# Attention over sixteen wavelengths with routed experts: moving one exponential to VectorE, the wavelength weights, a store order and a bias addition

## The reference

```python
xn = layernorm(x)
Q, K, V = (xn @ W + b for each of q, k, v), split into 16 heads of 8
for wl in range(16):                                  # wavelengths
    m = cos(phase_modulators[wl])                     # per head
    scores = (Q * m) @ (K * m).T / sqrt(8)
    scores = scores * cos(KERR * scores * scores)
    acc += softmax(scores) @ V * interference_weights[wl]
attention = (acc / 16) @ Wo + bo
# experts: each token goes to its best expert, if that has room
probs = softmax(xn @ gate_w.T)
expert_out[e] = relu(tokens_of_e @ w1[e] + b1[e]) @ w2[e] + b2[e]
out = x + attention + probs_of_choice * expert_out
```

## Time and profile before

| what | value |
|---|---|
| time, median of 3 runs | 1809.99 us (1807.09 to 1810.4) |
| the profiled execution | 1809.65 us, span 1807.9 us |
| ACT busy | 1726.9 us, 96% of the span |
| DVE busy | 1526.0 us, 84% |
| PE busy | 1490.7 us, 82% |
| POOL busy | 157.6 us, 9% |
| mean granted TensorE clock | 0.986 |
| exponentials of 128 x 4096 | 482, 3626 ns each |
| tails of 128 x 1024 on ScalarE | 8, 1041 ns each |

### The profile page before, as it was taken

The page is one execution under the profiler, slowest core; times in us unless marked ns, Lnnn a source line. Parts: engine busy times, 40 slices in busy tenths (PEclk is TensorE's granted clock), DMA queues, the critical chain, the costliest instruction groups (busy, mean ns, idle before and its releaser), DMA issues. The chain is left out here.

```text
span 1807.9 us, 45710 instructions
## 1 busy us (share of the span) xinstructions
PE 1490.7 (82%) x20014; PEld 942.5 (52%) x20014; DVE 1526.0 (84%) x2554; ACT 1726.9 (96%) x533; POOL 157.6 (9%) x168
## 2 busy tenths in 40 slices
PE   4797888777899999999997787777787787778877
PEld 2364544544556666656664454444455555445555
DVE  8445887889898888988888999999988998898785
ACT  3699999999999999999999999999999999999995
POOL 6200111110000000000000131332000000000000
PEclk9799999999999999999999999999999999999998
DMA  6000111000011110111000000000000000000001
GB/s 207 21 15 15 37 49 43 23 25 15 22 36 42 42 43 20 31 36 43 22 22 15 18 12 25 23 25 19 15 2 15 15 15 15 15 15 2 8 13 31
DMA packets 44999, 50.07 MB, mean 28 GB/s; under 512 B 6725, under 2 KB 37359, under 8 KB 44799
## 3 DMA queue, kind: packets, MB, share of 16 engines
q1 hardware_dynamic: 42463, 42.91, 7.5%
q0 software_dynamic: 2048, 4.20, 0.7%
q10 hardware_dynamic: 288, 0.00, 0.0%
HBM read 30.96 MB, written 15.73 MB: 26 GB/s over the span
## 5 line engine op out<-in xcount | busy, mean ns | idle before, releaser
L1044 ACT ACTIVATE Pr<-T 128x4096 f32<-128x4096 f32 x482 | 1694.3, 3626 | 17.7 <-PE bank L924 16.9
L924 PE MATMUL bank<-Pr,Vst 128*32 128x256 f32 x15424 | 936.7, 383 | 249.6 <-ACT Pr L1044 140.9
L924 PEld LDWEIGHTS bank<-Pr,Vst 128*32 128x32 f32 x15424 | 520.2, 110 | 546.8 <-issue 343.8
L866 DVE COPY T<-bank 128x512 f32<-128x512 f32 x252 | 172.4, 684 | 82.9 <-PE bank L860 82.9
L850 DVE TENSOR_REDUCE negmax<-bank 128x2 f32<-128x512 f32 x256 | 164.1, 681 | 30.1 <-PE bank L844 28.7
L1015 PE MATMUL bank_b<-terms,ident 128*128 128x128 f32 x1024 | 150.3, 280 | 0.8 <-DVE terms L1003 0.7
L965 DVE SCALAR_TENSOR_TENSOR d_mantissa<-d_mantissa 128x1024 f32<-128x1024 f32 x108 | 147.0, 1361 | 0.0
L968 DVE SCALAR_TENSOR_TENSOR shared<-shared,d_scaled 128x1024 f32<-128x1024 f32 x108 | 140.0, 1297 | 0.0
L1015 PEld LDWEIGHTS bank_b<-terms,ident 128*128 128x128 f32 x1024 | 130.3, 192 | 16.0 <-issue 9.1
L971 DVE SCALAR_TENSOR_TENSOR shared<-d_mantissa,shared 128x1024 f32<-128x1024 f32 x108 | 132.0, 1222 | 2.9
L963 DVE SCALAR_TENSOR_TENSOR shared<-d_mantissa 128x1024 f32<-128x1024 f32 x108 | 130.9, 1212 | 0.0
(11 more groups left out here) (175 smaller groups left out, 911.1 us busy)
## 6 DMA issues: line engine op xcount, KB each, us to landing
Ks<-qk_parts SPq DMA_DIRECT2D x31, 288.0 KB
Qs<-qk_parts SPq DMA_DIRECT2D x93, 96.0 KB
work<-in_L_ffn_w_dram SPq DMA_DIRECT2D x16, 256.0 KB, 3.5
qk_parts<-Pr SPq DMA_DIRECT2D x8, 384.0 KB, 2.7
qk_parts<-work SPq DMA_DIRECT2D x8, 384.0 KB, 2.8
dispatched<-T SPq DMA_DIRECT2D x5, 512.0 KB, 4.9
region<-dispatched SPq DMA_DIRECT2D x8, 320.0 KB, 3.5
expert_out<-work SPq DMA_DIRECT2D x8, 320.0 KB, 2.4
```

What stands on the lines that cost most here:

```text
L866: nc.vector.tensor_copy(T[par][:, ds(p * BANK, BANK)], sc_bank[rr][:, :]).then_inc(sc_read, 1)
L924: ins = nc.tensor.matmul(bank[VC * j:VC * (j + 1), half * SEQ:(half + 1) * SEQ], Vst[par][:, at:at + VC], moving, start=opens and half == ...
L1044: nc.scalar.activation(Pr[n % RING][:, :], T[par][:, :], ACT.Exp, scale=scales[u % 2][w]).then_inc(exp_done, 1)
```

## The change

1. `D_CHUNKS` is 4 in the units with an expert too. ScalarE's tail falls away there, VectorE gets seven more operations, and the products of wavelength 15 move behind the next unit's first products.
2. The wavelength weights go into the copies. A column of row_weight holds, for one group, 16 in each row of sums and the weight in each row of totals; row_scale is its reciprocal. The copy to pv_s becomes a multiplication by that column, the gain operation falls away. row_weight is filled at the start by GpSimd and by 16 small DMAs from ScalarE's queue.
3. SyncE issues the last part's store of units 2 and 3 after the next stack's load.
4. GpSimd adds the bias bo to base in four operations behind the first two stagings, no longer in the combine.

```diff
+    FIRST_OF = (0, 3, 6, 8, 11, 14)
+    LAST_OF = (2, 5, 7, 10, 13, 15)
...
+                    pool.memset(row_weight[:, :], float(W)).then_inc(weight_room, 1)
                     pool.memset(one_col[:, :], 1.0).then_inc(root_table, 1)
...
                     act.dma_start(bk_s[:, :], bk.rearrange("(d a) -> d a", a=1)).then_inc(bias_in, 16)
+                    act.wait_ge(weight_room, 1)
+                    for w in range(W):
+                        q = GROUP_OF[w]
+                        row = (w - FIRST_OF[q]) * OC + HD
+                        act.dma_start(row_weight[row:P:VC, q:q + 1], weights.rearrange("(a w) -> a w", a=1)[:, w:w + 1].to_broadcast([GR, 1])
+                                      ).then_inc(row_weight_in, 16)
...
+                    dve.wait_ge(row_weight_in, 16 * W)
+                    nc.vector.reciprocal(row_scale[:, :], row_weight[:, :])
...
+            def pool_output_bias(pool):
+
+                pool.wait_ge(xn1_ready, SIDE_TILES)
+                for c in range(CHUNKS):
+                    b = base[:, c * CH:(c + 1) * CH, :]
+                    nc.gpsimd.tensor_tensor(b, b, bo_s[:, :].unsqueeze(1).to_broadcast([P, CH, D]), ALU.add).then_inc(biased, 1)
...
             def pool_combine(pool, c):
-                nc.gpsimd.tensor_tensor(base[:, s, :], base[:, s, :], bo_s[:, :].unsqueeze(1).to_broadcast([P, CH, D]),
-                                        ALU.add).then_inc(pool_comb, 1)
+                pool.wait_ge(biased, CHUNKS)
                 pool.wait_ge(gathered[c], 16 * CH)
...
-                nc.vector.tensor_copy(pv_s[q % 2][:, :], pv_bank[q % 2][:, :]).then_inc(pv_copied, 1)
+                nc.vector.tensor_scalar(pv_s[q % 2][:, :], pv_bank[q % 2][:, :], row_scale[:, q:q + 1], None, ALU.mult).then_inc(pv_copied, 1)
...
-                nc.vector.tensor_tensor(gain[:, 0:size, :], rsum[:, 0:size, :], weight, ALU.mult).then_inc(gain_ready, 1)
-                dve.wait_ge(gain_ready, n + 1)
...
-                                        gain[:, 0:size, :].unsqueeze(3).to_broadcast([P, size, OTW, HD]), ALU.mult).then_inc(terms_ready, 1)
+                                        rsum[:, 0:size, :].unsqueeze(3).to_broadcast([P, size, OTW, HD]), ALU.mult).then_inc(terms_ready, 1)
...
-            D_CHUNKS = [{FIRST: 0, SECOND: 2, PLAIN: 4, EXPERT: 3, FINAL: 4}[KINDS[u // 2]] for u in range(UNITS)]
+            D_CHUNKS = [{FIRST: 0, SECOND: 2, PLAIN: 4, EXPERT: 4, FINAL: 4}[KINDS[u // 2]] for u in range(UNITS)]
...
                 for u in range(2):
                     stage_v(pool, u, u)
+                pool_output_bias(pool)
...
-                for u in range(2, 4):
+                for u in range(2, 5):
                     j = (u - 2) * NQ_SIDE
                     sp.wait_ge(sc_made, pair_no(u, 0))
                     load_stack(sp, u + 2, u % 2)
-                    sp_side1(sp, j, j + NQ_SIDE - 1)
+                    if u > 2:
+                        sp_side1(sp, j - 1, j)
+                    if u < 4:
+                        sp_side1(sp, j, j + NQ_SIDE - 1)
                     load_rows(sp, u + 2, u % 2)
-                    sp_side1(sp, j + NQ_SIDE - 1, j + NQ_SIDE)
-                for u in range(4, EU):
+                for u in range(5, EU):
                     unit(u, u % 2)
```

More of the change, by code:

```diff
@@ L71, in attention_and_experts @@
     RING = 2
+    FIRST_OF = (0, 3, 6, 8, 11, 14)
+    LAST_OF = (2, 5, 7, 10, 13, 15)
+    GROUPS = len(FIRST_OF)
+    GROUP_OF = tuple(sum(w > last for last in LAST_OF) for w in range(W))
     DCOLS = 4 * SEQ
@@ L144, in attention_and_experts @@
         rsum = sb("rsum", [P, SLOTS, OTW])
-        gain = sb("gain", [P, SLOTS, OTW])
+        row_weight = sb("row_weight", [P, len(FIRST_OF)])
+        row_scale = sb("row_scale", [P, len(FIRST_OF)])
         terms = [sb(f"terms{i}", [P, SLOTS, OTW * HD]) for i in range(2)]
@@ L229, in attention_and_experts @@
             proj, part1, rest1, part2, part3 = (ssem(n) for n in ("proj", "part1", "rest1", "part2", "part3"))
-            v_made = ssem("v_made")
+            v_made, weight_room, row_weight_in = ssem("v_made"), ssem("weight_room"), ssem("row_weight_in")
             angle, sine = ssem("angle"), ssem("sine")
@@ L508, in attention_and_experts @@
                 "v_staged", "exp_done", "pv_done", "pv_copied", "turned"))
-            inverted, gain_ready, terms_ready, terms_summed, summed = (asem(n) for n in (
-                "inverted", "gain_ready", "terms_ready", "terms_summed", "summed"))
+            inverted, terms_ready, terms_summed, summed = (asem(n) for n in (
+                "inverted", "terms_ready", "terms_summed", "summed"))
             exp_table, t0_copied, d_step, whole_done = asem("exp_table"), asem("t0_copied"), asem("d_step"), asem("whole_done")
@@ L518, in attention_and_experts @@
                 "route", "gate_in", "gate_exp", "mask_ready", "index_ready"))
-            scattered, pool_comb, base_ready = asem("scattered"), asem("pool_comb"), asem("base_ready")
+            scattered, pool_comb, base_ready, biased = asem("scattered"), asem("pool_comb"), asem("base_ready"), asem("biased")
             gathered = [asem(f"gathered{c}") for c in range(CHUNKS)]
@@ L773, in pool_combine @@
                 s = slice(c * CH, (c + 1) * CH)
-                nc.gpsimd.tensor_tensor(base[:, s, :], base[:, s, :], bo_s[:, :].unsqueeze(1).to_broadcast([P, CH, D]),
-                                        ALU.add).then_inc(pool_comb, 1)
+                pool.wait_ge(biased, CHUNKS)
                 pool.wait_ge(gathered[c], 16 * CH)
                 nc.gpsimd.tensor_tensor(got[:, s, :], got[:, s, :], over(r[:, 0, s], D), ALU.mult).then_inc(pool_comb, 1)
-                pool.wait_ge(pool_comb, 2 * (c + 1))
+                pool.wait_ge(pool_comb, c + 1)
                 nc.gpsimd.tensor_tensor(base[:, s, :], base[:, s, :], got[:, s, :], ALU.add).then_inc(base_ready, 1)
@@ L994, in dve_turned @@
                 slots = tr_bank[:, :].rearrange("p (a c) -> p a c", c=VC)[:, :, 0:size * OC].rearrange("p a (s c) -> p s a c", c=OC)
-                weight = over(iw_s[:, FIRST_OF[q]:LAST_OF[q] + 1], OTW)
                 dve.wait_ge(turned, n + 1 + 2)
@@ L1048, in stage_v @@
                                       .rearrange("p (t d) -> p t d", d=HD)).then_inc(v_staged, 1)
[L1052 to L1055, removed]
             COPY_AT = {3: 0, 6: 1, 8: 2, 11: 3, 14: 4, 17: 5}
@@ L1244, in plain_scalar @@
             def plain_scalar(act):
-                nc.scalar.activation(gain[:, 0, 0:1], one_col[:, :], ACT.Exp).then_inc(exp_table, 1)
+                nc.scalar.activation(rsum[:, 0, 0:1], one_col[:, :], ACT.Exp).then_inc(exp_table, 1)
                 for q in range(0, SIDE_B, 2):
```

## The result

The changed kernel takes 1786.38 us (median of 4 runs, 1786.15 to 1787.72) beside 1809.91 us for the kernel before (4 runs): ratio 0.9875, 95% interval 0.9858 to 0.9892. It is faster by 23.5 us; 20 were forecast, and the range 1784 to 1800 holds it. The profiled execution took 1786.21 us, its span 1784.5.

A forecast was written before the change was run, and what follows sets the result against it. Bound by ScalarE's exponentials, plus a start, an end and 24.7 us of breaks. 8.0 + 6.7 + 0.4 + 6.5 - 1.3 - 0.2 = 20.1 off 1809.99 gave 1789.9, written as 1790 us; range 1784 to 1800.

The forecast's parts named there:

- Stores behind loads: Units 3 and 4: loading the stack ahead of the store closes ScalarE's waits of 3.73 and 4.30 us; gain 8.0 us.
- Bias early: Combines: without GpSimd's bias addition, all four ScalarE breaks from 1105 us on go; gain 6.7 us.
- Rival 2: Combines: GpSimd's multiplication and addition still block VectorE, so the four breaks stay; 1796.6 us, chance 0.07.
- The bias at the start: Start: GpSimd's four bias additions delay VectorE's split of the row maxima, and so ScalarE's third exponential; cost 1.3 us.
- Sixteen DMAs at no cost: Setup: sixteen issues take 7.4 us, within ScalarE's 7.77 us idle before its first root; no cost, 0.4 us of cover spare.
- rival 3: Setup: the sixteen DMAs take 1.09 us each, making the first root 9.7 us late; 1799.6 us, chance 0.10.
- the prediction's own signs of being wrong: VectorE busy throughout an expert unit with TensorE waiting, first root after 11 us, or VectorE steps of several us under the combine.
- The whole last wavelength: Eight expert units: ScalarE's 1.04 us tail and 0.21 us wait go, a new 0.5 us wait comes at seven boundaries; gain 6.5.
- The total in front of them is the same: Expert unit boundaries: TensorE's reordered work ahead of the second products takes equally long, so a 0.5 us wait appears.
- rivals 1 and 4: Expert units: 1, VectorE binds, 1796.4 us, chance 0.14; 4, VectorE's 7.67 us idle does not shrink, 1843 us, chance 0.08.
- The end: Last two groups, behind the last exponential: VectorE's chain gets shorter through the weights in the copies; gain 0.4 us.
- The copies: VectorE, each group: the copy of 0.68 us becomes a multiplication by a per-partition scalar, 0.07 us more.

The follow-up runs named there:

- the reversal: The changed kernel with one part taken back: for the stores, SyncE's old order, 1795.42 us; for the last wavelength, three VectorE chunks in expert units, 1794.39 us.
- two kernels with the same start: The kernel before (1809.91 us) and the changed kernel with the weights where they were (1786.87 us); same code up to GpSimd's bias addition at 57.4.
- second profile: The changed kernel run once more without any change, as yardstick for three later kernels: 1786.86 us.
- the fourth kernel above: The changed kernel with DMA issues and reciprocal moved later, bias addition delayed, and 4, 2, 3, 3 chunks on VectorE in units 0 to 3: 1780.88 us.

## Why the prediction was right, point by point

- **Stores behind loads: 8.0 forecast.** 8.24 by the reversal. The load was forecast for 8.0 us before its unit's first exponential and went out 9.8 before it.
- **Bias early: 6.7.** All four breaks went, as forecast, and the bias did it alone. The term was a little small: the first exponentials of two such units stood 54.55 us apart (1159.75 - 1105.20 in the trace before), 1.9 more than fifteen exponentials of 3.51, while I counted the 1.72 that shows. Rival 2 (the two other instructions block as before) fell. The forecast's reason held for the step that it looked at: that step finds GpSimd idle, which waits for the gathered rows until 1112.62, and takes 1.22 us. The Trainium skill's SBUF — State Buffer (SBUF: two separate sides, under Who interferes with whom), which stands behind rival 2, is borne out all the same: the step at 1113.83 ends 1.1 us after GpSimd's multiplication does (1115.07). What the forecast and the rival both lacked is how long GpSimd works without a gap: bias and multiplication together had none, multiplication and addition have one, and so the two that are left block for 1.1 and 0.8 us and not for 3.9 and 2.2.
- **The bias at the start: -1.3.** The bias alone cost 0.90 (the wait ahead of the third exponential was 1.35 instead of 0.45); that the third exponential came 1.28 later in all, with 0.38 from the first in it, and so near 1.3, is chance. VectorE's cast of the maxima, 0.17 us, took 1.38, until GpSimd's addition ended at 67.50:

```profile
58.23 9.27 POOL L556 TENSOR_TENSOR base<-base,bo_s 128x1024 f32<-128x1024 f32 x4
...
66.15 1.38 DVE L893 CAST nm_parts<-negmax 128x16 bf16<-128x16 f32 x1
```

- **Sixteen DMAs at no cost.** This step was wrong in size. An issue took 0.57 us (9.14 / 16), not 0.45, so the first root came at 12.35 instead of 11.01: the cover of 0.4 us was gone, as rival 3 had it, but by 1.3 us and not by 9.7. A first root later than 11 us was one of the prediction's own signs of being wrong, and it came. Most of the 1.3 was taken up by later waits of the setup; the first exponential was 0.38 later, with the new reciprocal in it, for which 0.2 had been charged, and within the 0.46 by which two kernels with the same start differ (62.98 and 62.52, above). The 14 issues at 46.83 took 0.53 each with no issue of SyncE beside them, so most of the price is the issue's own. The Trainium skill's Perfetto Trace Analysis (Per-instruction lifecycle: what the profiler-reported window actually captures) has the generator locked by each issue; the runs do not clearly show that as a delay of SyncE: its three loads of x took 3.15 to 4.13 us in the five executions with the sixteen beside them and 3.01 to 3.45 in the five without.
- **The whole last wavelength: 6.5.** 7.63 by the reversal. The mechanism was right, wait and place included; the size of the new wait was off, 0.20 to 0.21 instead of 0.5. "The total in front of them is the same" failed: the same pieces take TensorE 0.29 us less in the new order. VectorE's busy time was 51.14 of 52.96 us where 52.1 was estimated, and its idle time shrank from 7.67 to 1.8: rivals 1 and 4 fell. With the gain in the chain it is 52.00, and 0.3 us of the wait at the boundary is left, so rival 1 was close.
- **The end: 0.4.** VectorE's chain there is 0.41 us shorter, as forecast. The span shows 1.26 (23.32 before, 22.06 after); the end varies by more than that from one execution to the next, see below.

The copies cost what was forecast, 0.741 us instead of 0.679 (0.06 more, forecast 0.07).

The forecast was 3.6 us too high: 1.1 from the last wavelength, 0.2 to 0.7 from the combine, 0.2 each from the stores and the start, 0.9 from the end; the rest is within the scatter of the runs. Only within the start do errors cancel (the bias 0.90 instead of 1.3, the first exponential 0.38 instead of 0.2); all else lies on the same side, and of that the 0.9 at the end is chance.

## What to carry over

Where one engine is busy to 96%, list its breaks in its own timeline, find the one late step behind each, and price the edits apart: here they added up to within 0.6 us. Before giving work to a second engine, ask whether its idle time is waiting in a fixed order or room; here the 5.6 us of the fourth chunk fitted into the 8.3 us that VectorE was idle without it (53.89 - 45.56). In this kernel VectorE lost 6.3 us under three GpSimd instructions of which the first two stood without a gap, and 1.9 under the two that were left: taking out one of 2.4 us freed 4.4.

## What was not expected of the hardware

The stretch behind the last exponential, nearly the same code in all of them, lasted from 21.69 to 23.65 us in ten profiled executions. TensorE's granted clock goes with it in part. The stretch in three windows (busy us of PE, PEld, DVE, ACT, POOL; then the clock, DMA share, GB/s), first in the changed kernel (22.06 us), then in its second profile (22.91):

```profile
1762.44:1770.44 8.00, 5.65 (x64) 3.76 (x56) 2.73 (x6) 0.00 (x0) 0.00 (x0) 1.00 0.01 2
1770.44:1776.44 6.00, 2.57 (x14) 2.30 (x15) 0.02 (x1) 1.10 (x2) 0.00 (x0) 0.84 0.02 5
1776.44:1784.50 8.06, 4.74 (x35) 4.55 (x34) 2.75 (x4) 1.20 (x2) 0.00 (x0) 0.91 0.43 130
```

```profile
1762.39:1770.39 8.00, 6.20 (x64) 4.58 (x56) 2.45 (x5) 0.00 (x1) 0.00 (x0) 0.88 0.01 2
1770.39:1776.39 6.00, 2.47 (x11) 2.06 (x11) 0.29 (x1) 0.89 (x2) 0.00 (x0) 0.50 0.02 5
1776.39:1785.30 8.91, 5.60 (x40) 5.41 (x39) 2.75 (x4) 1.50 (x3) 0.00 (x0) 0.87 0.39 118
```

TensorE has work for 6 of the first 8 us and for 2.5 of the next 6. In the second profile the clock fell within the first 8 us and stood at 0.50, the lower of its two levels (1.2 of 2.4 GHz), through the next 6; in the first it fell later. The three executions with 1.00 in the first window had 21.69, 21.83 and 22.06 us, the seven others, with 0.85 to 0.94, 22.69 to 23.65. The clock is not all of it: the kernel with the bias back in the combine and the fourth kernel above have the same clocks in the first two windows (0.85 and 0.78) and lasted 22.69 and 23.65 us. What places the fall of the clock, and what else lengthens the stretch, no experiment here shows. But two profiles can differ there by up to 2 us, so 0.4 us of gain at the end can't be read from the span.
